# Four graph layers on one core: the last half batch of each edge pass cut to the tiles that can hold edges

## The reference

```python
h = relu(layernorm(x))
# layer 0: sum at src of h[dst] * filter weight, then softplus(agg @ Wi1) @ Wi2
messages = x[col] * fsum
agg = segment_sum(messages, row)
# layer 1: two rounds of graph attention with one head
e = exp(leaky_relu(a_src[src] + a_dst[dst]) - m[dst])
msg = h[src] * (e / s[dst])
x_att = segment_sum(msg, dst)
# layer 2: a small network on each edge, mean at dst, a second one on each node
messages = linear(relu(linear([node_state[src], edge_state, global])))
# layer 3: graph attention with 8 heads of 16 features
out = segment_sum(h[src] * w, dst)
```

## Time and profile before

| | us |
|---|---|
| median of three runs | 7169.2 |
| the profiled execution | 7169.45 |
| its span, first to last instruction | 7167.7 |
| GpSimd busy | 4909.9 (68%) |
| TensorE busy with matmuls | 3252.6 (45%) |
| VectorE busy | 3183.8 (44%) |

### The profile page before, as it was taken

The page is one execution under the profiler, slowest core; times in us unless marked ns, Lnnn a source line. Parts: engine busy times, 40 slices in busy tenths (PEclk is TensorE's granted clock), DMA queues, the critical chain, the costliest instruction groups (busy, mean ns, idle before and its releaser), DMA issues. The chain is left out here.

```text
span 7167.7 us, 68724 instructions
## 1 busy us (share of the span) xinstructions
PE 3252.6 (45%) x17226; PEld 2905.4 (41%) x17226; DVE 3183.8 (44%) x9838; ACT 1647.9 (23%) x4158; POOL 4909.9 (68%) x5159
## 2 busy tenths in 40 slices
PE   5000001454444954444434444436767774444443
PEld 2000001444444944444434444435666663444443
DVE  8999511323233653333353333345333337444445
ACT  7000001222212832222233222223222223000000
POOL 2777776777777727777747777755777772777775
PEclk9555555666666975556566555557777777666666
DMA  6233333444444824444424444424444441444443
GB/s 248 95 115 115 116 114 102 160 160 162 156 162 163 279 79 132 131 134 132 131 89 133 132 133 132 133 80 127 136 135 136 134 131 58 131 135 130 134 130 108
DMA packets 509028, 957.63 MB, mean 134 GB/s; under 512 B 203945, under 2 KB 239104, under 8 KB 508515
## 3 DMA queue, kind: packets, MB, share of 16 engines
q1 hardware_dynamic: 350502, 645.51, 26.4%
q0 software_dynamic: 158144, 307.74, 16.6%
HBM read 678.19 MB, written 274.65 MB: 133 GB/s over the span
## 5 line engine op out<-in xcount | busy, mean ns | idle before, releaser
L1576 POOL DMA_INDIRECT edge_buf<-node_table,ixr x1664 | 1571.1, 944 | 614.6 <-issue 506.9
L1576 POOL DMA_INDIRECT Y<-node_table,ixr x1664 | 1570.4, 944 | 520.7 <-issue 517.6
L1260 DVE TENSOR_TENSOR ACC<-ACC,bank 128x129 f32 (+2 forms) x3328 | 973.0, 292 | 983.6 <-PE bank L1244 461.5
L1739 PE MATMUL bank<-adc,turned_buf 128*128 x2496 | 341.2, 195 | 1447.2 <-DVE z L1692 845.6
L1431 POOL DMA_INDIRECT layer_messages<-edge_buf,ixr x832 | 797.1, 958 | 292.3 <-issue 263.7
L459 POOL DMA_INDIRECT edge_records<-edge_buf x782 | 752.7, 963 | 255.7 <-issue 237.3
L1739 PEld LDWEIGHTS bank<-adc,turned_buf 128*128 128x128 bf16 x2496 | 256.6, 103 | 1579.3 <-issue 1526.3
L1244 PE MATMUL bank<-Y 128*128 128x129 f32 (+2 forms) x3328 | 751.7, 416 | 175.7 <-ACT Y L1725 102.6
L1244 PE MATMUL bank<-edge_buf,Y 128*128 128x129 f32 (+2 forms) x3328 | 757.7, 418 | 142.3 <-ACT edge_buf L1725 106.0
L1244 PEld LDWEIGHTS bank<-Y 128*128 128x128 f32 x3328 | 707.0, 319 | 198.9 <-issue 188.2
L1244 PEld LDWEIGHTS bank<-edge_buf,Y 128*128 128x128 f32 x3328 | 712.5, 322 | 164.1 <-issue 163.4
(11 more groups left out here) (311 smaller groups left out, 5179.6 us busy)
## 6 DMA issues: line engine op xcount, KB each, us to landing
Y<-onehots SPq DMA_DIRECT2D x416, 512.0 KB, 3.6
turned_buf<-onehots_turned SPq DMA_DIRECT2D x312, 256.0 KB, 3.9
edge_buf<-edge_records SPq DMA_DIRECT2D x208, 288.0 KB, 3.0
layer_messages<-ACC SPq DMA_DIRECT2D x28, 2112.0 KB
onehots<-Y SPq DMA_DIRECT2D x104, 512.0 KB
XI<-layer_messages SPq DMA_DIRECT2D x84, 528.0 KB, 4.7
edge_records<-H SPq DMA_DIRECT2D x1, 29952.0 KB, 79.5
onehots_turned<-turned_buf SPq DMA_DIRECT2D x104, 256.0 KB
```

The source lines that it names most:

```text
L1260: nc.vector.tensor_tensor(acc, acc, places.at(q, j, w), ALU.add).then_inc(added, 1)
L1576: pool.indirect_dma_start(ring[q][:, j, 0:w], None, table, bass.IndirectOffsetOnAxis(ap=ixr[q][:, j:j + 1], axis=0)).then_inc(rows_in[q], 16)
L1739: ins = nc.tensor.matmul(picks(q)[:, j * 6 * heads:(j + 1) * 6 * heads], ohbT[q][:, j * P:j * P + P], adc[:, bass.ds(at[j] * (6 * heads), ...
```

## The change

`tiles_in(n)` gives 8 tiles for half batches 0 to 102 and `LAST_TILES` = 829 - 824 = 5 for the last, 103. The last half batch of the destination pass scatters 5 tiles, and those of the four gathering passes gather, pick (attention passes), scale on ScalarE (one head), sum and add 5 tiles. Work that takes a half batch in one instruction (one-hot matrices, logits, L1698, L1808, L1840) stays as it is, and so do the transfers of one-hot matrices and records. In the source pass rounds stay 14, but half batches from `HALVES_S` = 110 on are left out: the last two of the last round, in places 6 and 7. The waits for the last half batch's transfers count 5 in place of 8.

```diff
@@ -43,10 +43,12 @@
 ITERS = NT // (2 * G)
+LAST_TILES = MAX_TILES - (NT - G)
 SLOTS = NT * P
...
 SLOTS_S = NTS * P
+HALVES_S = -(-2 * MAX_PAIRS // G)
 NTP = NT + G
@@ -67,6 +69,11 @@
 PI = 3.141592653589793
+
+
+def tiles_in(n):
+
+    return G if n < 2 * ITERS - 1 else LAST_TILES
@@ -1240,7 +1247,7 @@
                 pe.wait_ge(added, (n - places.sets + 1) * G)
-            for j in range(G):
+            for j in range(tiles_in(n)):
                 ins = nc.tensor.matmul(places.at(q, j, w), tiles_of_half(onehots)[:, j, :], messages[:, j, 0:w],
@@ -1426,13 +1433,13 @@
                             pool.sem_inc(poolt, 1)
-                            for j in range(G):
+                            for j in range(tiles_in(2 * i + h)):
...
                     for h in range(2):
-                        pool.wait_ge(sent[h], 16 * G * ITERS)
+                        pool.wait_ge(sent[h], 16 * (G * (ITERS - 1) + tiles_in(2 * ITERS - 2 + h)))
@@ -1455,6 +1462,10 @@
+            def halves_of(i, qs):
+
+                return [q for q in qs if i * deep + q < HALVES_S]
+
             def pair_at(q, j):
@@ -1463,7 +1474,7 @@
                     def body(i, first):
-                        for q in range(deep):
+                        for q in halves_of(i, range(deep)):
                             n = i * deep + q
@@ -1476,7 +1487,7 @@
                     def body(i, first):
-                        for q in others:
+                        for q in halves_of(i, others):
                             n = i * deep + q
@@ -1539,16 +1550,16 @@
                                 onehot_here(i, by_vector[0])
-                            for k in range(4):
+                            for k in (q - 4 * quad for q in halves_of(i, range(4 * quad, 4 * quad + 4))):
                                 add_pairs(n + k, 4 * quad + k, at[k * pairs:(k + 1) * pairs])
-                            if not quad:
+                            if not quad and by_vector[1] in halves_of(i, by_vector):
                                 onehot_here(i, by_vector[1])
...
                     def body(i, first):
-                        for q in range(deep):
+                        for q in halves_of(i, range(deep)):
                             n = i * deep + q
@@ -1572,7 +1583,7 @@
             pool.sem_inc(poolt, 1)
-            for j in range(G):
+            for j in range(tiles_in(r * DEEP + q)):
                 pool.indirect_dma_start(ring[q][:, j, 0:w], None, table,
@@ -1674,7 +1685,7 @@
                     def half(r, q, n):
-                        dve.wait_ge(rows_in[q], r * (16 * G) + 16 * G)
+                        dve.wait_ge(rows_in[q], r * (16 * G) + 16 * tiles_in(n))
                         if not known(n, 1):
```

## The result

The changed kernel takes 7139.59 us in the median of its first comparison (six of seven runs lie between 7137.53 and 7143.03), against 7168.66 us before (7167.17 to 7169.64). The ratio is 0.9959 [0.9949, 0.997]: 0.41% faster. The seventh run, the profiled one, took 7564.21 us at a mean granted clock of 0.576 in place of 0.65, and the ratio leaves it out. The forecast was 7139.6 us. The profile shown here is of the same kernel in the next comparison (7139.48 us, span 7137.8).

The account below looks back on a forecast made before the run. GpSimd's count of indirect DMAs was taken to bound the one-head passes, a VectorE-TensorE loop the eight-head pass. Savings of 3.8 + 3.6 + 14.6 + 4.8 + 3.0 = 29.8 us from 7169.45 gave 7139.6 us, range 7131 to 7149.

Parts of the forecast that it names:

- Destination pass: GpSimd's tail of the destination pass: three scatters fewer at 1.26 us each, 3.8 us saved.
- Source pass: End of the source pass: TensorE's last two half batches and their adds go, 3.6 us saved.
- One-head passes: Ends of both one-head passes: earlier gathers, shorter scaling, sum and adds save 7.3 us each, 14.6 us together.
- two level chains: One-head tail: TensorE's last sum allows the adds at 4786.14 us, VectorE is ready at 4786.21 us at worst.
- the second rival: One-head and layer 2 tails: earlier gathers come to nothing, 9.6 us lost, so 7149.2 us; chance 0.07.
- Layer 2's pass: Layer 2's tail: adds of half 102 start 2.17 us earlier, held by their sum; 4.8 us saved in all.
- Eight-head pass: Eight-head tail: earlier gathers buy nothing; picks 0.42, last sum 1.37 and last adds 1.23 us save 3.0 us.
- Everything else: Dense stages as long as before within 2 us each; the eight-head loop stays at 10.25 us a half.
- The high clock at the tails: Rival: last sums of four passes take 1.26 instead of 2.36 us, 4.4 us more gain, 7135.2 us; chance 0.10.

Follow-up runs that it names:

- Compute alone: Against the kernel before: only picks, scalings, sums and adds of the last half batch cut to five tiles; all gathers, scatters and source pass kept. 7159.99 us, ratio 0.9987.
- gathers_only: Against the kernel before: only the last half batch's gathers and scatters cut to five; row work stays at eight tiles, source pass at 112 half batches. 7157.89 us, ratio 0.9984.
- filler_again: Changed kernel plus 20 extra matmuls behind each half's sum in the eight-head pass, on a slower chip: 8498.44 us, kernel before 8523.46, ratio 0.9969.
- layer2_last_apart: Changed kernel plus separate PSUM places for layer 2's last sum and 20 eight-head filler matmuls, slower chip: 8553.08 us, kernel before 8575.26, ratio 0.9976.
- the three parts: Three kernels, each with one part of the change: fewer gathers and scatters 7157.89 us, five-tile compute 7159.99 us, 110 source half batches 7166.42 us; before 7168.77.

## Why the prediction was right

- *Destination pass*: 3.8 forecast, 4.1 measured. *Source pass*: 3.6, and 3.1 or 3.6; its tail is the 8.42 us chain of the earlier trace rows, and the half microsecond lies in the pass ahead of it. Two kernels that leave this pass alone are 0.3 us off either way.
- *One-head passes*: 7.3 forecast, 7.2 and 7.2. Compute alone gave 3.48 and 3.35 us for the 3.57 worked out, and what the whole has beyond it, 3.7 and 3.8 us, is the gathers' 3.74. The forecast of two level chains held to 0.1 us: VectorE ended the adds of half 102 at 4770.67 and would have been ready 0.64 us later, after its address registers, and TensorE's sum let it start 0.74 us later (4771.41). That the gathers' gain came to nothing (the second rival) is refuted by the whole; gathers_only came 1.1 us towards it for another reason, the late rows.
- *Layer 2's pass*: 4.8 forecast, 5.1; the sum of half 102, forecast at its old 3.81 us, took 3.56. The wait of the adds of half 102 for their sum appeared as worked out (1.20 us). The other wait of this tail, of the sum of half 103 for the adds of half 102, stood in the forecast as before, and a place of its own for the last sum removed it.
- *Eight-head pass*: 3.0 forecast, 2.3. This is the term that was mis-sized. The last sum went from 3.66 to 2.60 us, 1.06 in place of 1.37. The 3.66 us of the earlier trace rows were partly at the high clock (the half before it took 3.97 us at a granted 0.50, this one was granted 0.56 from 7135 to 7139), the new 2.60 us were all at 0.50, and I took 3/8 of a mixed duration. The adds gave 1.29 for 1.23. The picks fell from 1.13 to 0.72 us, but the sum behind them started only 0.25 us nearer to the picks' start and took 3.97 in place of 3.83 us, so 0.11 of the 0.42 us are left.
- *Everything else*: the dense stages moved by 1.0 us in all, none by more than 0.6, and the loop kept 10.25 us. The passes give 29.0 and the dense stages 1.0 of the 29.9 us between the spans.
- *The high clock at the tails* didn't come: the five-tile sums took 2.49 to 2.60 us, the low level's. On the slower chips it came in both one-head tails of filler_again and in layer 2's tail of layer2_last_apart (1.35 us for five tiles each), so it can. It would have been worth less than the 4.4 us that the prediction gives this rival, which counts 1.1 us in each of four passes: in the one-head passes VectorE is level with TensorE in the prediction's own working, and in filler_again's tails the last adds start 0.55 us after those of half 102, on VectorE's own pace, against 0.74 us here. So some 0.2 us are to be had there, and 2.6 us in all.

The medians of the three parts are 7.3 us short of the whole (22.0 for 29.3). That is no contradiction, since each ratio's interval is 6 to 10 us wide on either side, and the lengths of the passes say more. Each part taken in the passes that it edits: gathers 3.66 + 2.63 + 2.65 + 2.78 = 11.72 us, compute 3.48 + 3.35 + 2.60 + 1.92 = 11.35, source 3.58, in all 26.65 us. With the 2.2 us of the two late landings that is 28.9, and the six passes of the whole give 29.0. The rest of the difference lies in stretches that the parts don't touch, and these move between executions: by up to 2.1 us in the table, and by 1.5 us ahead of the first scatter in compute alone.

## What to carry to other kernels

Work cut from the last step of a pipelined pass is worth its price on each engine in turn, as long as the chain through the step before doesn't end later: write down for each engine when it is done with the step before, and count the gain only up to there. Stages that an edit doesn't touch moved by up to 2 us between the profiled executions, so judge an edit of a few us by the length of its own pass and not by the total. If two sums in a row share a place, try a place of its own for the last one: in layer 2's tail that took away about 2 us, seen in the tail and not in the total. And before you read a landing from the first instruction behind the last gather, count which half it belongs to and look whether its engine was idle.

## What was not expected of the hardware

- A 16 KB transfer of an instruction queue holds up one of a gather's 16 row packets until it ends: in 96 of 96 gathers that met one, the last packet ended after 2.6 to 3.1 in place of 2.2 us. Within a pass the gathers kept their 1.248 us all the same; on the last gather it went with a landing 1.1 to 1.2 us later (3.60 and 3.71 in place of 2.5 us). No run moved such a transfer on purpose.
- The same kernel takes 7169 us on one chip and 8523 to 8579 us in three comparisons on others, with instructions equally long (0.94 us a gather on both). All of the difference lies in stretches with indirect DMAs, in waits between instructions, VectorE's own chain among them. The cause isn't shown.
- More activity lifted the mean granted clock from 0.58 to 0.66 and 0.72, and the sums on the path didn't get shorter for it (median 3.96 us each time).
